# Rotary embedding without a rotation matmul: permuted query and key weight columns in a fused two-layer kernel

## The chip, the cores and the metric

The kernel runs on one core of one Trainium2 chip. The metric is device time in microseconds (us) of one execution, as a median of several. The engines are TensorE (PE, its weight loads PEld), VectorE (DVE), ScalarE (ACT), GpSimd (POOL) and SyncE (SP), which issues the transfers.

## The reference

A first layer blends a memory into the stream; a second one is a transformer layer with two experts per token (self attention, cross attention, feed forward). What the change touches is the projection to queries, keys and values and the rotary embedding (B = 4 batches of S = 512 tokens, D = 512, 16 heads of 32):

```python
vm = expert_mask(token_type_ids)[..., None]
x = rms_norm(hidden_states, ln_in_w)
mixed = jnp.where(vm, x @ v_qkv, x @ l_qkv)
q, k, v = jnp.split(mixed, 3, axis=-1)
q, k, v = (heads(q, NH, HD), heads(k, NH, HD), heads(v, NH, HD))
# rotate_half(x) = concatenate([-x[..., d:], x[..., :d]]), d = 16
q, k = q * cos + rotate_half(q) * sin, k * cos + rotate_half(k) * sin
ctx = sdpa(q, k, v, causal=True)
```

## The kernel before

The whole model is one program on one core, cut into stages by an all-engine barrier (`clear`, L71 to L76): gated_context (L89), queries_values_keys (L689), self attention (from L1143), projections, cross attention, feed forward. Each engine has its own instruction stream, written out by hand in the order in which it runs; semaphores order the engines against each other. Matrix products are made of float32 values split into a rounded high part and a rest: three matmuls per product (`three`, L104 to L108).

The stage queries_values_keys works on one batch per turn, four turns (`turns`, the last batch first). In a turn TensorE runs three phases of eight steps, four for expert 0 and four for expert 1 (`project` and `run`): Q (part 0), V (part 1), K (part 2); the last turn has the order Q, K, V (`place`). A phase fills four of the eight PSUM banks, so that a phase's banks are written again two phases later. Q and K come out transposed, one piece of 128 output features x 512 tokens per bank; V has tokens on the partitions. Expert 1 is computed only for the last 128 tokens if no early token needs it: after the fourth step of Q, TensorE reads a flag and branches (L1138 to L1141) to a wide or a narrow version of the rest of the turn; with these inputs the narrow one runs, and the wide one, which lies before it in the program, is jumped over.

After the fourth step of Q two matmuls (`sums`, L1105) add the squares of the tokens for the norms of the turn. ScalarE makes the roots (`root`), VectorE the scaled tables cos_r and sin_r (`second_sums` L995 and L998, `tables` L1004 to L1007). TensorE's V phase waits for the second of these steps (s_tab at 5i + 2).

The rotary embedding of a piece goes through five engines. ScalarE copies the piece out of PSUM (`keep_plain`, L840). GpSimd multiplies the copy by cos_r (`scale_pieces`, L931), TensorE multiplies it by a constant matrix rot that swaps the halves of each head with the sign (`rotate`, L1097; one matmul in plain float32, four records in the trace, back into the piece's own bank). VectorE multiplies that by sin_r (L1017) and adds both (L1020). ScalarE rounds the sum (`round_piece`, L847; two slots), VectorE takes the rest (L1024), and SyncE stores both (`store_piece`, L754 and L756) as 128 rows of 2 KB. The products with cos_r lie in a ring t1 of three slots. On TensorE the rotations of a turn's Q pieces stand behind the first two steps of its V phase, two per step, and those of its K pieces behind the first two steps of the next turn's Q phase; in the last turn Q's stand in the K phase and K's in the V phase.

VectorE's order in a turn is: `turn_pieces` for the preceding turn's K, `second_sums`, `tables`, `turn_pieces` for this turn's Q, the copy rs_col (L1050) of four transposed columns that TensorE makes at V's fifth step (L1130), then masks, tokens and rests of the next turn (`find_keep`, `mask_x`, `rest_x` L987). The K phase waits for rs_col. In turn 0 the splits of the key weights (`round_w` on ScalarE, `rest_w` on VectorE) stand among these. The query weights of expert 0 are split at the end of the stage before (`split_tile`, L357 to L370).

## Time and profile before

| what | value |
|---|---|
| timed runs | 2179.99, 2180.31 and 2183.4 us, median 2180.31 us |
| profiled execution, span | 2183.6 us |
| TensorE busy | 2022.3 us (93%) |
| VectorE busy | 1492.5 us (68%) |
| ScalarE busy | 1006.7 us (46%) |
| GpSimd busy | 503.2 us (23%) |
| the stage queries_values_keys, from Q's expert 1 of turn 0 to the next stage's first matmul | 389.53 to 623.39 us |

All rows come from one execution that was profiled; for that execution the profile gives the span and no other time. Busy times count work, not waiting. Matmuls are pipelined, their ends are modelled and overlap the following starts, so distances between starts are read rather than durations. PEclk is the clock that TensorE was granted, as a share of full speed. A bracket behind a row gives the idle time of that engine just before it and what ended it. "PEq" and "PEldq" are TensorE's sequencer, "SPq" the queue of SyncE.

### The profile page before, as it was taken

How to read it: one execution, taken by the hardware profiler on the slowest of the kernel's cores; microseconds unless marked ns; L12 is line 12 of the kernel's file. 1: busy time of each engine (PE TensorE's matmuls, PEld its weight loads, DVE VectorE, ACT ScalarE, POOL GpSimd, SP SyncE). 2: the span in 40 equal slices, each digit the busy share in tenths (PEclk: the TensorE clock that was granted, in tenths of full speed). 3: DMA queues.
4: the chain of work that ended last, by engine and by line, in shares of the span. 5: the costliest groups of instructions: out<-in, count | busy, mean ns of one | idle time of the engine just before them, and what ended most of it. 6: DMA issues, size and time to landing. Idle time of an engine off the chain costs nothing. (4 is left out here: it accounts for less than half of the span.)

```text
span 2183.6 us, 32815 instructions
## 1 busy us (share of the span) xinstructions
PE 2022.3 (93%) x12701; PEld 1349.4 (62%) x12718; DVE 1492.5 (68%) x2047; ACT 1006.7 (46%) x1748; POOL 503.2 (23%) x496
## 2 busy tenths in 40 slices
PE   6999997899979997888889999999998899999997
PEld 5788874677755554677634444444434678778885
DVE  5776786566547775656579999999952565866563
ACT  1333314445415554444348888888884222221111
POOL 0321231133301212332201213222132212221211
PEclk9999998799979999999979999999999899999999
DMA  3222112333367662585544354453501433344332
GB/s 139 70 99 80 40 53 86 113 122 122 99 173 171 171 166 87 207 263 195 156 124 84 71 97 83 78 98 69 97 17 26 124 88 102 98 110 112 99 94 58
DMA packets 174936, 236.99 MB, mean 109 GB/s; under 512 B 26234, under 2 KB 103166, under 8 KB 172570
## 3 DMA queue, kind: packets, MB, share of 16 engines
q1 hardware_dynamic: 166624, 223.71, 38.2%
q0 software_dynamic: 7856, 10.90, 1.8%
q8 instruction: 113, 1.85, 0.4%
q14 instruction: 55, 0.45, 0.1%
q10 hardware_dynamic: 288, 0.08, 0.0%
HBM read 169.61 MB, written 62.91 MB: 106 GB/s over the span
## 5 line engine op out<-in xcount | busy, mean ns | idle before, releaser
L2133 ACT ACTIVATE pT_x<-ps 128x512 f32<-128x512 f32 (+1 forms) x832 | 451.3, 595 | 85.3 <-PE ps L2231 57.6
L2172 DVE TENSOR_REDUCE quarters<-ps 128x2 f32<-128x804 f32 x480 | 454.4, 992 | 46.1 <-PE ps L2203 45.0
L2246 PE MATMUL ps<-pT_x,vx_ring 128*17 128x256 f32 (+1 forms) x3328 | 261.9, 388 | 0.2 <-ACT osb_x L2115 0.2
L106 PE MATMUL ps<-mi_h,w_hi 128*128 128x512 f32 (+1 forms) x440 | 174.0, 396 | 10.5 <-DVE mi_l L2427 10.5
L2392 POOL TENSOR_TENSOR sg<-sg,keep_all 128x512 f32<-128x512 f32 (+1 forms) x55 | 87.8, 1595 | 386.5 <-ACT sg L2371 386.5
L107 PE MATMUL ps<-mi_h,w_lo 128*128 128x512 f32 (+1 forms) x440 | 173.4, 394 | 0.0
L108 PE MATMUL ps<-mi_l,w_hi 128*128 128x512 f32 (+1 forms) x440 | 172.8, 393 | 0.0
L1320 DVE TENSOR_REDUCE row_max_s<-ps 128x1 f32<-128x384 f32 (+3 forms) x176 | 109.5, 633 | 67.9 <-PE ps L1352 67.1
L1292 ACT ACTIVATE pT_s<-ps 128x512 f32<-128x512 f32 (+1 forms) x176 | 96.0, 558 | 114.9 <-PE ps L1377 112.8
L100 DVE CAST w_hi<-w_raw 128x512 fp32r<-128x512 f32 (+1 forms) x165 | 84.4, 511 | 71.5 <-PE ps L108 65.5
L2246 PEld LDWEIGHTS ps<-pT_x,vx_ring 128*17 128x17 f32 (+1 forms) x3328 | 55.6, 95 | 110.9 <-issue 68.5
L102 DVE TENSOR_TENSOR w_lo<-w_raw,w_hi 128x512 fp32r<-128x512 f32 (+1 forms) x165 | 115.8, 702 | 5.7
L2375 ACT ACTIVATE hid_h<-prod 128x512 fp32r<-128x512 f32 (+1 forms) x55 | 34.9, 634 | 177.5 <-DVE prod L2455 177.5
L2371 ACT ACTIVATE sg<-ps 128x512 f32<-128x512 f32 (+1 forms) x55 | 32.8, 596 | 164.4 <-PE ps L108 164.4
L291 ACT ACTIVATE pT<-ps 128x512 f32<-128x512 f32 (+1 forms) x52 | 31.0, 598 | 158.0 <-PE ps L108 158.0
L106 PEld LDWEIGHTS ps<-mi_h,w_hi 128*128 128x128 f32 (+1 forms) x440 | 82.3, 187 | 31.0 <-issue 11.5
L1352 PE MATMUL ps<-qkv_h,qkv_l 96*128 96x128 f32 (+3 forms) x256 | 90.5, 414 | 10.1 <-PEq L76 7.8
L108 PEld LDWEIGHTS ps<-mi_l,w_hi 128*128 128x128 f32 (+1 forms) x440 | 82.3, 187 | 20.1
L107 PEld LDWEIGHTS ps<-mi_h,w_lo 128*128 128x128 f32 (+1 forms) x440 | 82.3, 187 | 18.8
L2455 DVE TENSOR_TENSOR prod<-ps,sg 128x512 f32<-128x512 f32 (+1 forms) x55 | 37.9, 690 | 78.8 <-PE ps L108 70.0
L106 PE MATMUL ps<-hid_h,w_hi 128*128 128x512 f32 (+1 forms) x220 | 87.9, 400 | 3.0 <-DVE hid_l L2459 3.0
L331 POOL TENSOR_TENSOR sin_t<-sin_t,pT 128x512 f32<-128x512 f32 (+1 forms) x48 | 72.4, 1509 | 65.0 <-ACT pT L291 64.4
(350 smaller groups left out, 4816.6 us busy)
## 6 DMA issues: line engine op xcount, KB each, us to landing
qkv_l<-self_q_by_part SPq DMA_DIRECT2D x48, 256.0 KB, 4.5
qkv_h<-self_k_by_part SPq DMA_DIRECT2D x48, 256.0 KB, 6.6
w_raw<-L_xattn_l_gate SPq DMA_DIRECT2D x40, 256.0 KB, 2.9
w_raw<-L_xattn_l_up SPq DMA_DIRECT2D x40, 256.0 KB, 2.9
w_raw<-L_xattn_l_down SPq DMA_DIRECT2D x40, 256.0 KB, 2.7
kx_first<-cross_k_by_part SPq DMA_DIRECT2D x36, 200.2 KB, 6.7
cross_v_by_group<-v_aug SPq DMA_DIRECT2D x16, 442.0 KB, 3.8
vx_ring<-cross_v_by_group SPq DMA_DIRECT2D x16, 442.0 KB, 10.0
```

The lines of the kernel that those rows point to most:

```text
L100: nc.vector.tensor_copy(hi, raw).then_inc(s_high, 1)
L102: nc.vector.tensor_tensor(out=lo, in0=raw, in1=hi.bitcast(f32), op=ALU.subtract).then_inc(s_split, 1)
L106: nc.tensor.matmul(dst, ah, bh, start=start, stop=False, **how)
L107: nc.tensor.matmul(dst, al, bh, start=False, stop=False, **how)
L108: return nc.tensor.matmul(dst, ah, bl, start=False, stop=stop, **how)
L1292: nc.scalar.activation(pT[:, u % 3, j:j + n, 0:width], heads_of(ps[:, SCORES + v % 3, :], n, width), ACT.Exp, scale=SCALE).then_inc(s["s_e ...
L1320: nc.vector.tensor_reduce(out=row_max[:, g % 2, j:j + heads, q], in_=heads_of(bank, heads, (q + 1) * P), axis=AX.X, op=ALU.max)\
L1352: last = nc.tensor.matmul(bank[:, m * width:(m + 1) * width], q_r[0:STACK, at + m, cut], k_r[0:STACK, at + m, 0:width], start=False, stop= ...
L2133: nc.scalar.activation(pT[0:kn, u % 3, j, :], ps[0:kn, 5 + v % 3, :], ACT.Exp, scale=SCALE)\
L2172: nc.vector.tensor_reduce(out=quarters[:, g % 2, pair, :, q, quarter], in_=ps[:, at:at + 2, 0:MAXW], axis=AX.X, op=ALU.max)\
L2246: last = nc.tensor.matmul(ps[j * HD:j * HD + CHD + 1, 4, queries], v_r[0:kn, g % RING, kt, j, :], pT[0:kn, u % 3, j, queries], start=kt == ...
L2392: nc.gpsimd.tensor_tensor(out=by_batch(sg[0:cn, c % 2, :]), in0=by_batch(sg[0:cn, c % 2, :]), in1=keep_all[0:cn, experts[i], :, rows(i)], ...
```

## The change

The columns of the query and key weights are permuted when the weights are split into high part and rest. Piece q then holds, for all eight pairs of heads, one half of one head of the pair: pieces 0 and 1 hold the first and second halves of the even heads, pieces 2 and 3 those of the odd heads. What the rotation matmul fetched from 16 partitions further is now in the same partition of the neighbouring bank (j and j ^ 1). VectorE multiplies piece j by cos_r and piece j ^ 1 by sin_r, both straight from PSUM; GpSimd subtracts or adds the two; ScalarE rounds as before, VectorE takes the rest, two pieces behind instead of one. `keep_plain`, `rotate`, the constant rot and its load are gone. The ring t1 has four slots, and VectorE, not GpSimd, now waits for a free slot. A piece is stored as eight blocks of 16 rows, so that the rows in memory are in the old order. The `sums` of a turn and the transposes at V's fifth step wait for the second multiply of two pieces. The value weights keep their order.

```diff
+        def by_piece(w):
+
+            return w.rearrange("p (a q r) -> p q a r", q=DT, r=HD // 2)
...
-                            nc.vector.tensor_copy(hi, w_raw[:, n % RAW, :]).then_inc(s["s_wh"], 1)
+                            raw = w_raw[:, n % RAW, :]
+                            if n >= DT + ET:
+                                raw, hi, lo = by_piece(raw), *(w.rearrange("p (q a r) -> p q a r", q=DT, r=HD // 2) for w in (hi, lo))
+                            nc.vector.tensor_copy(hi, raw).then_inc(s["s_wh"], 1)
                             dve.wait_ge(s["s_wh"], n + 1)
-                            nc.vector.tensor_tensor(out=lo, in0=w_raw[:, n % RAW, :], in1=hi.bitcast(f32), op=ALU.subtract)\
+                            nc.vector.tensor_tensor(out=lo, in0=raw, in1=hi.bitcast(f32), op=ALU.subtract)\
...
+            TR = 4
...
+                def piece_rows(dst, i, part, j):
+
+                    return dst[turns[i], part].rearrange("(a q r) n -> q a r n", q=DT, r=HD // 2)[j]
+
+                def raw_of(n):
+
+                    raw = w_raw[:, n % RAW, :]
+                    return raw if n // G == 1 else by_piece(raw)
+
+                def as_raw(w, n):
+
+                    return w if n // G == 1 else w.rearrange("p (q a r) -> p q a r", q=DT, r=HD // 2)
...
-                            sp.dma_start(dst[turns[i], 0, k * P:(k + 1) * P, :], hi[:, o % 2, :].bitcast(f32)).then_inc(s_uh[o % 2], 16)
+                            sp.dma_start(piece_rows(dst, i, 0, k), hi[:, o % 2, :].bitcast(f32)).then_inc(s_uh[o % 2], 16)
                             sp.wait_ge(s["s_rl"], o + 1)
-                            sp.dma_start(dst[turns[i], 1, k * P:(k + 1) * P, :], t1[:, o % 3, :]).then_inc(s_ul[o % 3], 16)
+                            sp.dma_start(piece_rows(dst, i, 1, k), t1[:, o % TR, :]).then_inc(s_ul[o % TR], 16)
...
-                            nc.scalar.activation(split_of(n)[0], w_raw[:, n % RAW, :], ACT.Copy).then_inc(s["s_wh"], 1)
+                            nc.scalar.activation(as_raw(split_of(n)[0], n), raw_of(n), ACT.Copy).then_inc(s["s_wh"], 1)
...
-                        def keep_plain(i, group):
-
-                            act.wait_ge(s["s_wu"], done(i, 2 * group))
-                            for j in range(DT):
-                                o = 2 * DT * i + DT * group + j
-                                if o >= DT:
-                                    act.wait_ge(s["s_rp"], o - DT + 1)
-                                nc.scalar.activation(plain[:, j, :], ps[:, bank(3 * i + place(i, 2 * group), j), :], ACT.Copy).then_inc(s["s_pl"], 1)
-
                         def round_piece(o):
 
                             act.wait_ge(s["s_rp"], o + 1)
                             if o >= 2:
                                 act.wait_ge(s_uh[o % 2], 16 * (o // 2))
-                            nc.scalar.activation(hi[:, o % 2, :], t1[:, o % 3, :], ACT.Copy).then_inc(s["s_rh"], 1)
+                                act.wait_ge(s["s_rl"], o - 1)
+                            nc.scalar.activation(hi[:, o % 2, :], t1[:, o % TR, :], ACT.Copy).then_inc(s["s_rh"], 1)
...
-                                keep_plain(i - 1, 1)
                                 for j in range(2):
                                     round_piece(2 * DT * (i - 1) + DT + j)
                             root(i, 0)
@@ -890,14 +900,12 @@
                                 for j in range(2, DT):
                                     round_piece(2 * DT * (i - 1) + DT + j)
                             root(i, 1)
-                            keep_plain(i, 0)
                             if i == 0:
                                 for n in range(2 * G, 3 * G):
                                     round_w(n)
                             for j in range(DT):
                                 round_piece(2 * DT * i + j)
                             if i == B - 1:
-                                keep_plain(i, 1)
...
-                        def scale_pieces(i, group):
-
-                            pool.wait_ge(s["s_tab"], 5 * (i + 1))
+                        def join_pieces(i, group):
+
                             for j in range(DT):
                                 o = 2 * DT * i + DT * group + j
-                                pool.wait_ge(s["s_pl"], o + 1)
-                                if o >= 3:
-                                    pool.wait_ge(s_ul[o % 3], 16 * (o // 3))
-                                nc.gpsimd.tensor_tensor(out=t1[:, o % 3, :], in0=plain[:, j, :], in1=cos_r[:, :], op=ALU.mult)\
-                                    .then_inc(s["s_t1"], 1)
+                                pool.wait_ge(s["s_t1"], o + 1)
+                                pool.wait_ge(s["s_t2"], o + 1)
+                                nc.gpsimd.tensor_tensor(out=t1[:, o % TR, :], in0=t1[:, o % TR, :], in1=plain[:, j, :],
+                                                        op=ALU.add if j % 2 else ALU.subtract).then_inc(s["s_rp"], 1)
...
+                            nc.vector.tensor_tensor(out=as_raw(lo_, n), in0=raw_of(n), in1=as_raw(hi_.bitcast(f32), n), op=ALU.subtract)\
...
                         def turn_pieces(i, group):
 
                             dve.wait_ge(s["s_tab"], 5 * (i + 1))
-                            for j in range(DT + 1):
+                            dve.wait_ge(s["s_wu"], done(i, 2 * group))
+                            for j in range(DT + 2):
                                 o = 2 * DT * i + DT * group + j
                                 if j < DT:
-                                    dve.wait_ge(s["s_rot"], o + 1)
-                                    dve.wait_ge(s["s_t1"], o + 1)
-                                    nc.vector.tensor_tensor(out=plain[:, j, :], in0=ps[:, bank(3 * i + place(i, 2 * group), j), :], in1=sin_r[:, :],
-                                                            op=ALU.mult).then_inc(s["s_t2"], 1)
-                                    dve.wait_ge(s["s_t2"], o + 1)
-                                    nc.vector.tensor_tensor(out=t1[:, o % 3, :], in0=t1[:, o % 3, :], in1=plain[:, j, :], op=ALU.add)\
-                                        .then_inc(s["s_rp"], 1)
-                                if j:
-                                    dve.wait_ge(s["s_rh"], o)
-                                    nc.vector.tensor_tensor(out=t1[:, (o - 1) % 3, :].bitcast(f32r), in0=t1[:, (o - 1) % 3, :],
-                                                            in1=hi[:, (o - 1) % 2, :].bitcast(f32), op=ALU.subtract).then_inc(s["s_rl"], 1)
+                                    banks = [ps[:, bank(3 * i + place(i, 2 * group), n), :] for n in (j, j ^ 1)]
+                                    if o >= TR:
+                                        dve.wait_ge(s_ul[o % TR], 16 * (o // TR))
+                                    nc.vector.tensor_tensor(out=t1[:, o % TR, :], in0=banks[0], in1=cos_r[:, :], op=ALU.mult)\
+                                        .then_inc(s["s_t1"], 1)
+                                    if o >= DT:
+                                        dve.wait_ge(s["s_rp"], o - DT + 1)
+                                    nc.vector.tensor_tensor(out=plain[:, j, :], in0=banks[1], in1=sin_r[:, :], op=ALU.mult)\
+                                        .then_inc(s["s_t2"], 1)
+                                if j >= 2:
+                                    dve.wait_ge(s["s_rh"], o - 1)
+                                    nc.vector.tensor_tensor(out=t1[:, (o - 2) % TR, :].bitcast(f32r), in0=t1[:, (o - 2) % TR, :],
+                                                            in1=hi[:, (o - 2) % 2, :].bitcast(f32), op=ALU.subtract).then_inc(s["s_rl"], 1)
...
-                        def rotate(i, group, j):
-
-                            o = 2 * DT * i + DT * group + j
-                            pe.wait_ge(s["s_pl"], o + 1)
-                            nc.tensor.matmul(ps[:, bank(3 * i + place(i, 2 * group), j), :], rot[:, :], plain[:, j, :], start=True, stop=True)\
-                                .then_inc(s["s_rot"], 1)
-
                         def sums(i, n):
 
                             pe.wait_ge(s["s_sum"], 3 * (2 * i + n + 1))
                             if i:
-                                pe.wait_ge(s["s_t2"], 2 * DT * (i - 1) + DT + n + 1)
+                                pe.wait_ge(s["s_t2"], 2 * DT * (i - 1) + DT + 2)
                             nc.tensor.matmul(ps[:, bank(3 * i + 1, n), :], ones[:, :], sq[:, 2 + n, :], start=True, stop=True)\
                                 .then_inc(s["s_ss"], 1)
 
@@ -1109,22 +1111,13 @@
 
                             parts = (0, 2, 1) if i == B - 1 else (0, 1, 2)
                             for m in steps:
-                                step, n = m % G, G * parts[m // G] + m % G
+                                n = G * parts[m // G] + m % G
                                 project(i, n, t0)
-                                if m < 2 and i:
-                                    rotate(i - 1, 1, 2 * m)
-                                    rotate(i - 1, 1, 2 * m + 1)
                                 if m == 3:
                                     sums(i, 0)
                                     sums(i, 1)
-                                if m // G == 1 and step < 2:
-                                    rotate(i, 0, 2 * step)
-                                    rotate(i, 0, 2 * step + 1)
-                                if i == B - 1 and m // G == 2 and step < 2:
-                                    rotate(i, 1, 2 * step)
-                                    rotate(i, 1, 2 * step + 1)
                                 if n == G + 4:
-                                    pe.wait_ge(s["s_t2"], 2 * DT * i + DT * (place(i, 1) - 1) + 1)
+                                    pe.wait_ge(s["s_t2"], 2 * DT * i + DT * (place(i, 1) - 1) + 2)
```

## Rows read from the trace of the kernel before

**Rows 1.** The page: busy us, share of the span and instructions of each engine.

```profile
PE 2022.3 (93%) x12701; PEld 1349.4 (62%) x12718; DVE 1492.5 (68%) x2047; ACT 1006.7 (46%) x1748; POOL 503.2 (23%) x496
```

**Rows 2.** Windows: length, busy (x) of PE, PEld, DVE, ACT, POOL, PEclk, DMA share, GB/s.

```profile
399.80:439.17 39.37, 37.53 (x173) 29.90 (x174) 28.51 (x40) 19.39 (x33) 10.21 (x8) 0.93 0.42 141
439.17:496.74 57.57, 56.85 (x283) 44.54 (x282) 37.97 (x53) 28.53 (x45) 19.95 (x15) 1.00 0.33 116
496.74:554.30 57.56, 56.83 (x283) 44.56 (x282) 37.95 (x52) 28.55 (x45) 19.96 (x15) 1.00 0.33 115
554.30:615.60 61.30, 60.59 (x290) 45.91 (x289) 33.12 (x45) 23.01 (x36) 20.24 (x15) 1.00 0.41 134
615.60:623.39 7.79, 0.04 (x1) 0.05 (x2) 0.00 (x0) 2.42 (x4) 0.00 (x0) 0.82 0.47 139
...
422.50:425.90 3.40, 3.40 (x10) 2.61 (x9) 2.20 (x5) 0.01 (x1) 0.00 (x0) 0.52 0.77 236
```

**Rows 3.** Lines, 399.8 to 616: busy us, mean ns of one, then idle before.

```profile
L1097 PE MATMUL ps<-plain,rot 128*128 128x512 f32 x64 | 30.7, 602 | 2.2 <-ACT plain L840 2.2
```

**Rows 4.** Timeline of TensorE, turn 0, V: start us, us, engine, line, operation.

```profile
402.55 0.39 PE L107 MATMUL ps<-qkv_h,xe0l 128*128 128x512 f32 x1
...
403.69 1.88 PE L1097 MATMUL ps<-plain,rot 128*128 128x512 f32 x4
...
405.64 0.40 PE L107 MATMUL ps<-qkv_h,xe0l 128*128 128x512 f32 x1
```

**Rows 5.** Timeline of TensorE, turn 1: Q, sums, V, V's expert 1, K.

```profile
439.46 0.40 PE L107 MATMUL ps<-xe0h,w_lo 128*128 128x512 f32 x1
...
441.80 0.40 PE L108 MATMUL ps<-xe0l,w_hi 128*128 128x512 f32 x1
...
454.67 1.88 PE L1105 MATMUL ps<-sq,ones 128*128 128x512 f32 x4
...
461.70 0.46 PE L106 MATMUL ps<-qkv_h,xe0h 128*128 128x512 f32 x1
...
476.63 0.39 PE L106 MATMUL ps<-qkv_h,xe1h 128*128 128x512 f32 x1
...
480.55 0.39 PE L106 MATMUL ps<-xe0h,qkv_h 128*128 128x512 f32 x1
```

**Rows 6.** Timeline of TensorE, turn 0: the first matmul of K.

```profile
421.30 0.47 PE L106 MATMUL ps<-xe0h,qkv_h 128*128 128x512 f32 x1 [1.83 <-DVE rs_col L1050]
```

**Rows 7.** Branch and first narrow instruction (ns min/median/max, starts); turn 0's Q, expert 1.

```profile
L1139 PEldq COMPARE_BRANCH  x4: 3312/3530/3811, 382.3 to 567.4; - x4
...
L1068 PEldq EVENT_SEMAPHORE  x4: 51/51/51, 389.4 to 393.4; - x4
...
389.53 0.44 PE L106 MATMUL ps<-xe1h,qkv_h 128*128 128x128 f32 x1 [6.37 <-issue]
```

**Rows 8.** Lines of the pieces' steps on VectorE, GpSimd and ScalarE, 330 to 640.

```profile
L1020 DVE TENSOR_TENSOR t<-t,plain 128x512 f32<-128x512 f32 x32 | 25.8, 807 | 1.1
...
L1017 DVE TENSOR_TENSOR plain<-ps,sin_r 128x512 f32<-128x512 f32 x32 | 21.9, 685 | 32.6 <-POOL t L931 23.9 <-PE ps L1097 8.7
...
L931 POOL TENSOR_TENSOR t<-plain,cos_r 128x512 f32<-128x512 f32 x32 | 43.7, 1386 | 104.2 <-DVE sin_r L1007 39.8 <-ACT plain L840 27.3 <-DMA self_q_by_part<-t 22.0
...
L847 ACT ACTIVATE rows_h<-t 128x512 fp32r<-128x512 f32 x32 | 19.8, 629 | 54.9 <-DVE t L1020 54.9
```

**Rows 9.** Timeline of VectorE, turn 2: last rest of x, last table.

```profile
499.20 1.53 DVE L987 TENSOR_TENSOR xe1l<-full_x,xe1h 128x512 fp32r<-128x512 f32 x1 [0.16 <-ACT xe1h L820]
...
523.23 0.68 DVE L1007 TENSOR_TENSOR sin_r<-sin_t,rs 128x512 f32<-128x512 f32 x1
```

**Rows 10.** Transfers, 340 to 640: count, size, median us to landing.

```profile
self_q_by_part<-rows_h SPq DMA_DIRECT2D x16, 256.0 KB, 2.3
...
qkv_h<-self_k_by_part SPq DMA_DIRECT2D x10, 256.0 KB, 6.8
```

**Rows 11.** Timeline of VectorE, end of the stage before.

```profile
331.21 1.29 DVE L498 COPY h<-ps 128x512 f32<-128x512 f32 x2 [1.79 <-PE ps L108]
```

More of the change, by code:

```diff
@@ L236, in _ @@
                             load_w(sp, n, tiles[n], wl, s["s_ws"])
-                        sp.wait_ge(s["s_pos"], 96)
+                        sp.wait_ge(s["s_pos"], 80)
                         sp.wait_ge(s["s_up"], 16 * (B - 1))
@@ L392, in positions @@
                         def positions():
-                            dve.wait_ge(s["s_pos"], 96)
+                            dve.wait_ge(s["s_pos"], 80)
                             nc.vector.tensor_copy(posf, posi).then_inc(s["s_hot"], 1)
@@ L689, in queries_values_keys @@
         def queries_values_keys(more_h, more_l, k_r, q_r, v_r, s_key, s_value, s_first):
[L691 to L692 removed]
+            names = ("s_tt s_k s_ku0 s_ku1 s_eu s_hin s_x s_xh s_xl s_sq s_sum s_ss s_rs s_tab s_r0u s_t1 s_t2 s_rp s_rh s_rl "
+                     "s_uh0 s_uh1 s_ul0 s_ul1 s_ul2 s_ul3 s_rc s_rcc s_vn s_uv0 s_uv1 s_hup " + WSEMS)
             ctx, sems = stage(names)
@@ L695, in queries_values_keys @@
             wl = [s[f"s_wl{i}"] for i in range(RAW)]
-            s_ku, s_uv, s_uh, s_ul = ([s[f"{n}{i}"] for i in range(k)] for n, k in (("s_ku", 2), ("s_uv", 2), ("s_uh", 2), ("s_ul", 3)))
+            TR = 4
+            s_ku, s_uv, s_uh, s_ul = ([s[f"{n}{i}"] for i in range(k)] for n, k in (("s_ku", 2), ("s_uv", 2), ("s_uh", 2), ("s_ul", TR)))
             weights, GROUPS, G = [t["L1_xattn_l_qkv"], t["L1_xattn_v_qkv"]], (0, 2, 1), 2 * DT
@@ L783, in _ @@
                                     sp.wait_ge(s_uv[m], 16 * ST)
-                                for m in range(3):
-                                    sp.wait_ge(s_ul[m], 16 * len(range(m, 4 * DT, 3)))
+                                for m in range(TR):
+                                    sp.wait_ge(s_ul[m], 16 * len(range(m, 4 * DT, TR)))
                                 self_key_loads(sp, 0, k_r, q_r, s_key)
@@ L803, in _ @@
                             sp.wait_ge(s_uh[m], 16 * DT * B)
-                        for m in range(3):
-                            sp.wait_ge(s_ul[m], 16 * len(range(m, 2 * DT * B, 3)))
+                        for m in range(TR):
+                            sp.wait_ge(s_ul[m], 16 * len(range(m, 2 * DT * B, TR)))
                     @block.scalar
@@ L936, in _ @@
                             if i:
-                                scale_pieces(i - 1, 1)
-                            scale_pieces(i, 0)
+                                join_pieces(i - 1, 1)
+                            join_pieces(i, 0)
                             if i + 1 < B:
                                 add_squares(i + 1)
-                        scale_pieces(B - 1, 1)
+                        join_pieces(B - 1, 1)
                     @block.vector
@@ L967, in rest_w @@
                             dve.wait_ge(s["s_wh"], n - SPLIT + 1)
-                            nc.vector.tensor_tensor(out=lo_, in0=w_raw[:, n % RAW, :], in1=hi_.bitcast(f32), op=ALU.subtract)\
+                            nc.vector.tensor_tensor(out=as_raw(lo_, n), in0=raw_of(n), in1=as_raw(hi_.bitcast(f32), n), op=ALU.subtract)\
                                 .then_inc(s["s_ws"], 1)
@@ L2573, in constants @@
     c = {"c_ident": np.eye(P, dtype=np.float32)}
-    rot = np.zeros((P, P), np.float32)
-    low = p % HD < HD // 2
-    rot[p[low] + HD // 2, p[low]] = -1.0
-    rot[p[~low] - HD // 2, p[~low]] = 1.0
-    c["c_rot"] = rot
     c["c_sel"] = (p[:, None] == np.array([[HD * h for h in range(4)] + [HD * h + CHD for h in range(4)]])).astype(np.float32)
```

6 lines of the change are left out of this document (1 added, 5 removed).

## The prediction

> **What bounds the kernel now.** I read the page's busy times first: TensorE is busy for 2022.3 of the 2183.6 us span, VectorE for 1492.5 [rows 1]. That is an average over stages, so I then cut the one stage that the change rebuilds (queries, values, keys) into its four turns, at each turn's first matmul. The reader is to see the TensorE column: 56.85 of 57.57 us and 56.83 of 57.56 in turns 1 and 2, at full granted clock, with VectorE at 38 and GpSimd at 20 [rows 2]. So TensorE's stream sets the end of every turn, and what leaves that stream is gained if nothing else becomes later than it. The grouped lines give the stream's share that goes: 64 records of the rotation matmul, 30.7 us busy, 2.2 us idle before them waiting for ScalarE's copies [rows 3]. The rows in order of time then give the price in the stream (ends of pipelined matmuls overlap, so I use distances between starts).
>
> **The change part by part.**
>
> *Rotations removed.* Plain matmuls start 0.228 us apart (402.55 to 403.69 is five of them). From the first rotation record at 403.69 to 405.64 are 1.95 us, with one plain matmul inside: a pair of rotations costs 1.95 − 0.23 = 1.72 us [rows 4]. There are 16 pairs (two in turn 0, four in turns 1 and 2, six in turn 3): 16 x 1.72 = 27.5 us. Pairs that also wait cost more; to catch that I build a turn without rotations. Expert 0 of Q is 48 matmuls at 0.234 (439.46 to 441.80 is ten of them): 11.2. From the sums to V's start, 454.67 to 461.70: 7.0. Expert 0 of V, 48 x 0.228: 10.9. V's expert 1 with the transposes, 476.63 to 480.55: 3.9. K, 480.55 to the next turn's first matmul at 496.74: 16.2 [rows 2, 5]. Sum 49.3 against 57.57: **8.2 us in each of turns 1 and 2**, of which 6.9 are pairs and 1.3 their waits. Turn 3 is the same work in another order, and its window ends 0.3 us after its last start: 61.30 − 49.3 − 0.3 = **11.6 us**.
>
> *Turn 0.* Two pairs, 3.4 us. K's first matmul stood 1.83 us for the copy rs_col [rows 6], which is queued on VectorE behind the Q pieces, and these behind the K weights' splits. ScalarE's four copies that stood ahead of those splits are gone, so the splits run while TensorE still works on Q's expert 1; the pieces begin at Q's end (399.8) and need about 9 us, while V takes 14.8. The stall goes: 1.8 us. After it the granted clock fell for 3.4 us to 0.52, that is near 1.2 of 2.4 GHz [rows 2]: (1 − 0.52) x 3.4 = 1.6 us that I expect back, since nothing stands there any more. Last the jump, L1139: the branch over the wide version of the turn takes 3.3 to 3.8 us in all four turns; in turns 1 to 3 the matmuls already queued cover it, in turn 0 TensorE stood 6.37 us, and its stream's first narrow instruction came at 389.4, 7 us after the branch began at 382.3 [rows 7]. So there two waits of that size follow one another. Fewer instructions per turn put the turn's code elsewhere; from 7.1 − 3.8 the second wait is worth up to 3.3 us. Ends 0 and 3.3; I take 1.5, the middle, having no nearer row. Turn 0 in all: 3.4 + 1.8 + 1.6 + 1.5 = **8.3 us**.
>
> *The pieces' new path.* Per piece VectorE did multiply by sin, add, rest; now it does two multiplies from PSUM and the rest: three again. The old multiply reads PSUM too and takes 685 ns [rows 8], so the new ones take that, at 0.62 from start to start: nothing gained or lost in busy time, if two PSUM operands from neighbouring banks cost no more. GpSimd does one operation per piece as before (1386 ns, two SBUF operands, as the join [rows 8]). ScalarE loses 32 copies. What matters is when each wait of TensorE is met.
> K pieces wait only for VectorE: the preceding turn's last x rest ends at 499.20 + 1.53 = 500.73, 4.0 us after the turn's start [rows 2, 9]. The second pair of multiplies, for which sums now wait, ends at 4.0 + 4 x 0.62 = 6.5; sums come at 11.2. Covered by 4.7 us. If that cover were gone, TensorE would wait there with the whole turn behind it.
> Q pieces begin when the tables are done, 523.23 + 0.68 = 523.91 in turn 2; I call this T. V starts at 461.70 + 57.56 = 519.26 in that turn, T − 4.65, so without rotations K starts at T − 4.65 + 10.9 + 3.9 = T + 10.2 [rows 2, 5, 9]. Behind T: multiplies of three pieces to T + 3.7; joins from 1.3 in steps of 1.39 to T + 5.5 for three, the fourth 7.0; piece 1 is rounded by T + 4.8 (0.63 on ScalarE [rows 8]), its store then needs 2.3 us to land [rows 10] before the same slot is rounded for piece 3: T + 7.1, rounded 7.8, rest done 8.6, rs_col 8.8. It is needed at T + 10.2. So **1.4 us of cover**, the thinnest of the change. Gone, it costs its excess in turns 1 and 2.
> The slot wait of the t1 ring moves from GpSimd to VectorE; queued behind it there are the other pieces and rs_col. With four slots it asks for a store issued a whole group earlier: nothing.
>
> *Stores* now write 8 blocks of 16 rows instead of 128 rows, from the same queue, as many as before. The nearest row is the old store, 2.3 us; the far one 6.8 us, a load of the same size [rows 10]. I take 2.3; up to 3.7 nothing is late.
>
> *Weight columns.* Reads of the raw tile in short runs, in 16 splits. The 12 of this stage lie beside TensorE work. Four in the stage before are VectorE casts of 0.42 us, back to back with work for which TensorE waits (1.79 us before L498's copies, 0.65 each [rows 11]). If the short runs cost the cast its speed, 4 x (0.65 − 0.42) = 0.9 us are lost; ends 0 and 0.9, I take **0.4 us lost**. One constant load less: off the path, nothing.
>
> *Sum.* 8.3 + 8.2 + 8.2 + 11.6 − 0.4 = **35.9 us**. The next stage starts 7.79 us after the last window in any case [rows 2]: a barrier, all later work moves as one. The profiled execution's span, 2183.6 us, is 0.2 above the slowest of the timed runs and 3.3 above their median, 2180.31; the rows differ from a timed run by 0.15%, on 36 us nothing. Forecast: 2180.3 − 35.9 = **2144.4 us**.
>
> **The rivals.**
>
> *rs_col comes late.* For: two operations with two SBUF operands now meet oftener, the join on GpSimd and the rest on VectorE, and such VectorE operations are the uneven ones: L1020's mean is 807 ns against 685 for L1017 with one PSUM operand, and one rest beside GpSimd took 1.53 [rows 8, 9]. Against: during most of a join VectorE runs PSUM multiplies. If all four rests took 1.53, the last ends 3.4 us later, 2.0 beyond the cover; with a clock dip as in turn 0, 3.6 a turn, in two turns 7 us: 2151.5.
> The Trainium skill, "GPSIMD Engine Reference", section 1. Specifications, says that GpSimd shares its SBUF interfaces with VectorE and contends with VectorE instructions of two SBUF inputs. By that rule this rival holds in part; the trace agrees in the direction (807 against 685 ns), and the new multiplies are of the kind that it spares.
>
> *The double wait at the jump moves to another turn.* For: code moves in every turn. Against: a turn's waits have to fall together as in turn 0. Then turn 0's 1.5 may turn to 3.3 and another turn pays 3.3 and a dip of 1.6: 2144.4 − 1.8 + 4.9 = 2147.5, or, where turn 0 keeps its own too, 2151.
> The Trainium skill, "Runtime: NRT & Kernel Launch", section Instruction fetch mechanics, says that a taken branch to code outside two 16 KiB blocks forces a fetch before it goes on. By that the second wait would depend on where a block ends; the trace shows the 3.3 to 3.8 us per jump, not the blocks' place in the changed program.
>
> *Slower: the stores land late.* Each group of four pieces has one landing between rounding piece 1 and piece 3. Above 3.7 us every microsecond of landing delays K's start in turns 1 and 2; above some 5 (tables behind the K pieces' last rest) also V's start in turns 1 to 3; turn 0 and the end follow later. With some six groups on the path the loss is about 6L − 26: 6.8 us (the far row) would cost 15 and leave 2159; the sign turns at L near 10.5, and 12 us would give 2190. Blocks of 32 KB speak against so much.
>
> *Nothing gained.* If the pieces' chain replaced TensorE as the bound, a turn would be as long as VectorE's 38 us plus its waits; it would need 11 us of waits to reach 49.3 and 19.5 for today's time [rows 2]; VectorE has 19.6 of idle now, most of it on the rotation's chain. 2180.
>
> **How the numbers follow.** Forecast 0.76, late rs_col 0.10, jump 0.08, late stores 0.04 (half of it with a loss), nothing gained 0.02. Range: below, the jump's second wait wholly gone (−1.8), no cast loss (−0.4), and up to 1.5 for unevenness that the dense turn of plain distances leaves out: 2140.7. Above, the two middle rivals: 2152. A measurement of this kernel can tell about 0.2% (4 us) from no change. Faster 0.95, same 0.02, slower 0.03.
>
> **What would show it.** In the profile after: no L1097; turns 1 and 2 at 49 to 50 us with TensorE over 98% busy; turn 3 near 49.6; no idle before K's first matmul in turn 0 and no low clock behind it; less than 6.4 us of "issue" before Q's expert 1 there; stores landing within 3.7 us. I am wrong if a turn's K starts behind rs_col, if a jump shows a gap in turns 1 to 3, or if the multiplies take over 0.7 us.

## The result: 18.9 us faster, half of what was forecast

The changed kernel takes 2162.0 us (median of four runs, 2161.4 to 2164.3), the kernel before 2180.9 beside it: a ratio of 0.9911, with a 95% interval of 0.9898 to 0.9925. The forecast was 2144.4 us with a range of 2140.7 to 2152.0: the sign was right, the size was not, 35.9 us against 18.9.

The page's busy times after the change:

```profile
PE 1989.5 (92%) x12637; PEld 1334.6 (62%) x12654; DVE 1482.1 (69%) x2047; ACT 991.2 (46%) x1716; POOL 507.3 (23%) x496
```

TensorE has lost 32.8 us of busy time against [rows 1], ScalarE 15.5 us; its 32 copies are gone. The work went, then; the time didn't all follow. The windows by turn, cut as in [rows 2] (turn 0 from V on, turns 1 to 3, the way to the next stage), and a short one behind K's start in turn 2 (length; busy and count of PE, PEld, DVE, ACT, POOL; PEclk; DMA share; GB/s):

```profile
397.21:429.99 32.78, 32.78 (x166) 27.74 (x166) 21.74 (x33) 12.62 (x21) 10.67 (x8) 0.95 0.34 114
429.99:481.21 51.22, 49.61 (x267) 41.58 (x266) 33.69 (x49) 22.86 (x34) 20.62 (x14) 1.00 0.40 129
481.21:536.72 55.51, 51.73 (x267) 42.69 (x266) 38.16 (x56) 26.17 (x39) 21.30 (x15) 0.97 0.37 120
536.72:586.35 49.63, 49.63 (x266) 41.53 (x265) 29.08 (x43) 16.36 (x22) 22.22 (x15) 1.00 0.45 132
586.35:600.46 14.11, 0.00 (x2) 0.06 (x2) 1.46 (x3) 3.68 (x6) 0.00 (x0) 0.58 0.59 193
518.79:524.00 5.21, 5.21 (x16) 4.13 (x17) 3.32 (x8) 1.21 (x2) 0.00 (x0) 0.67 0.73 219
```

Turn 3 has the forecast length (49.63 us against 49.3 + 0.3). Turn 1 is 1.9 us too long, turn 2 6.2 us, and from the last V matmul to the next stage are 14.11 us instead of 7.79 [rows 2]. These three make 14.4 of the 17 us that are missing. TensorE's own rows say what it stood for (timeline of TensorE: K of turns 0 and 1, V of turn 2, K of turn 2):

```profile
413.80 0.39 PE L105 MATMUL ps<-xe0h,qkv_h 128*128 128x512 f32 x1
...
464.93 0.47 PE L105 MATMUL ps<-xe0h,qkv_h 128*128 128x512 f32 x1 [1.61 <-DVE rs_col L1059]
...
501.45 0.50 PE L105 MATMUL ps<-qkv_h,xe0h 128*128 128x512 f32 x1 [1.11 <-DVE rs L1004]
...
518.79 0.47 PE L105 MATMUL ps<-xe0h,qkv_h 128*128 128x512 f32 x1 [2.24 <-DVE rs_col L1059]
```

The stall of [rows 6] is gone in turn 0. New ones stand in front of K in turns 1 and 2, at the place that the prediction called the thinnest cover of the change, and one in front of V in turn 2, for the tables. Behind the one of 2.24 us the granted clock is 0.67 in the mean of 5.2 us (the last window): 1.7 us more.

Why rs_col is late is read in the chain of turn 2's Q pieces, step by step against the prediction's times behind T, the end of the tables (timeline of VectorE, ScalarE and SyncE's queue; L858 rounds a piece, L773 issues the store of its high part):

```profile
505.47 0.68 DVE L1013 TENSOR_TENSOR sin_r<-sin_t,rs 128x512 f32<-128x512 f32 x1
...
510.20 0.63 ACT L858 ACTIVATE rows_h<-t 128x512 fp32r<-128x512 f32 x1 [0.62 <-POOL t L937]
...
511.37 0.56 SPq L773 DMA_DIRECT2D self_q_by_part<-rows_h  x1
...
517.22 0.63 ACT L858 ACTIVATE rows_h<-t 128x512 fp32r<-128x512 f32 x1 [2.80 <-DMA self_q_by_part<-rows_h]
...
518.49 0.15 DVE L1059 COPY rs_col<-ps 128x4 f32<-128x4 f32 x1
```

T is 506.15. Piece 1 is rounded at T + 4.7 (forecast T + 4.8). Its store is issued 0.5 us later, at 511.37, and the slot is free for piece 3 only at 517.22, 5.85 us after the issue, where the forecast had 2.3. Everything after is late by about that: rs_col is done at T + 12.5 instead of T + 8.8, K starts at T + 12.6 instead of T + 10.2.

The stores are the same 256 KB from the same queue. In the transfers' table they have no landing time any more (compare [rows 10]):

```profile
self_q_by_part<-rows_h SPq DMA_DIRECT2D x16, 256.0 KB
```

The reason lies in the trace's completion events. A store of the kernel before raised its semaphore 16 times, one of the changed kernel 9 times: once 1 us after the issue, then 8 times when data has landed. Taking the ninth event as the landing, the 64 stores took 4.06 us at best and 5.2 in the median; before they took 2.0 and 2.3. The Trainium skill, "DMA: Bandwidth & Descriptors", section "Why a DMA increments its semaphore by 16 and not by 1", gives the rule: a transfer from such a queue is shared by as many of the 16 DMA engines, at most, as divide the size of the slowest loop of both access patterns, and the queue writes the rest of the 16 counts at once. Eight blocks of 16 rows have a slowest loop of 8. By that rule eight engines carry what sixteen carried; the nine events and the doubled time agree. The prediction did not draw on this page.

### The profile page after: what moved, and what is told of

Its sections match the earlier page's. It is cut to its first block and busy times, and to the rows that moved or that the text cites. A ratio compares the mean times of both kernels' runs of the same rounds, so it can differ in the third digit from the quotient of the medians.

```text
span 2162.6 us, 32626 instructions
## 1 busy us (share of the span) xinstructions
PE 1989.5 (92%) x12637; PEld 1334.6 (62%) x12654; DVE 1482.1 (69%) x2047; ACT 991.2 (46%) x1716; POOL 507.3 (23%) x496
## 5 line engine op out<-in xcount | busy, mean ns | idle before, releaser
L106 PEld LDWEIGHTS ps<-mi_h,w_lo 128*128 128x128 f32 (+1 forms) x440 | 82.3, 187 | 18.6
```

Of the source, the lines that this page charges most:

```text
L106: nc.tensor.matmul(dst, al, bh, start=False, stop=False, **how)
```

## The experiments

**Is it the stores?** Two runs, each with the stores alone as the difference. In the first the kernel before gets the new blocks:

```diff
-sp.dma_start(dst[turns[i], 0, k * P:(k + 1) * P, :], hi[:, o % 2, :].bitcast(f32)).then_inc(s_uh[o % 2], 16)
+sp.dma_start(dst[turns[i], 0].rearrange("(a q r) n -> q a r n", q=DT, r=HD // 2)[k], hi[:, o % 2, :].bitcast(f32)).then_inc(s_uh[o % 2], 16)
...
```

> The kernel before with one edit: every piece is stored as 8 blocks of 16 rows (the rows then lie in another order in memory; nothing else is changed). Theory S (stores): such a store is finished by fewer DMA engines and lands in 4 to 6 us instead of 2.3, whatever the rest of the kernel does. In the kernel before the Q pieces have about 1.9 us to spare ahead of K's start in turns 1 and 2, so about 1 us a turn is lost there, with a clock dip after each stall, and the last turn's K pieces end late: 2180.5 + 4 to 10, about 2187. Theory C (contention): what is late in the changed kernel is late because GpSimd's joins and VectorE's rests slow each other, the store only stands in the row; then this edit costs under 2 us, 2181.

Measured: 2208.1 us against 2182.4, ratio 1.0115 (1.0091 to 1.0139): 25.7 us slower, two and a half times the upper end of what theory S expected, and far from theory C. The waits of the span 360 to 640 show where the rest is (engine, tile, line, waited for: us in total, times, longest):

```profile
POOL t L931 <- DMA self_q_by_part<-t: 38.2, 6, 14.4
...
POOL t L931 <- DMA self_k_by_part<-t: 27.9, 4, 7.9
```

I had counted the two slots of the high part alone. In the kernel before, GpSimd waits at the head of the pieces' path for a slot of the ring of three; in [rows 8] 22.0 us of its idle time already stood against that landing. Tables, copies and the rotations in TensorE's stream queue behind it.

In the second run the changed kernel gets the old block:

```diff
-return dst[turns[i], part].rearrange("(a q r) n -> q a r n", q=DT, r=HD // 2)[j]
+return dst[turns[i], part, j * P:(j + 1) * P, :]
```

> The changed kernel, but every piece is stored as one block of 128 rows as before the change (the rows then lie in another order in memory). Theory S: landings fall back to 2 to 2.4 us, the stalls at K's start in turns 1 and 2 (1.6 and 2.2 us) and what follows them go: turns 1 and 2 at 49.3 us instead of 51.2 and 55.5, 8 us gained; if the late tail (14.1 us from the last V matmul to the next stage instead of 7.8) is of the same cause, 6 more: 2148 to 2154. Theory C: the stalls stay, 2160 or more.

Measured: 2146.8 us, 35.6 less than the kernel before beside it (2182.4), ratio 0.9839 (0.9817 to 0.9861). The forecast's sum was 35.9. Turns 1 and 2 and the way to the next stage (windows), then the end of turn 2's tables, the rounding of piece 3 and rs_col (timeline), then the store's landing (transfers):

```profile
429.51:479.39 49.88, 49.60 (x266) 41.55 (x266) 36.91 (x52) 24.63 (x37) 21.01 (x15) 1.00 0.38 133
479.39:528.94 49.55, 49.55 (x267) 41.56 (x266) 37.21 (x53) 24.77 (x37) 20.63 (x15) 1.00 0.38 134
...
579.04:586.77 7.73, 0.00 (x1) 0.06 (x2) 0.00 (x0) 2.34 (x4) 0.00 (x0) 0.67 0.47 140
```

```profile
501.64 0.69 DVE L1013 TENSOR_TENSOR sin_r<-sin_t,rs 128x512 f32<-128x512 f32 x1
...
509.87 0.63 ACT L858 ACTIVATE rows_h<-t 128x512 fp32r<-128x512 f32 x1 [1.15 <-POOL t L937]
...
511.14 0.16 DVE L1059 COPY rs_col<-ps 128x4 f32<-128x4 f32 x1
```

```profile
self_q_by_part<-rows_h SPq DMA_DIRECT2D x16, 256.0 KB, 2.3
```

T is 502.33. rs_col is done at T + 9.0 (forecast 8.8) and K starts at 512.75, T + 10.4 (10.2). No K stands: theory C falls.

**Is it the number of blocks?** Two more kernels change that number alone. Four blocks of 32 rows:

```diff
-return dst[turns[i], part].rearrange("(a q r) n -> q a r n", q=DT, r=HD // 2)[j]
+return dst[turns[i], part].rearrange("(a q r) n -> q a r n", q=DT, r=HD)[j]
```

> The changed kernel with pieces stored as 4 blocks of 32 rows (the rows then lie in another order in memory). Theory S: half as many engines share a store as with 8 blocks, so a store alone lands in about 8 us instead of 4.1, and the slot waits of ScalarE and VectorE grow by 3 to 4 us a pair: each of turns 1 to 3 longer by 8 to 15 us, in all 2185 to 2215. If the number of blocks did not matter: 2162.

Measured: 2222.6 us, ratio 1.0186 (1.0168 to 1.0204), slower than the kernel before and above the expected range. At best a store lands in 6.1 us, not 8, with five events instead of nine. K now waits for 6.0 and 4.7 us in turns 1 and 2, and the second phase of turns 2 and 3 for the tables, 2.3 us each (timeline of TensorE, K of turn 1, V and K of turn 2); `sums`, which the prediction had seen covered, wait 6.9 us in turns 1 to 3 together:

```profile
483.63 0.76 PE L105 MATMUL ps<-xe0h,qkv_h 128*128 128x512 f32 x1 [5.99 <-DVE rs_col L1059]
...
530.13 0.79 PE L105 MATMUL ps<-qkv_h,xe0h 128*128 128x512 f32 x1 [2.29 <-DVE rs L1004]
...
552.51 0.53 PE L105 MATMUL ps<-xe0h,qkv_h 128*128 128x512 f32 x1 [4.67 <-DVE rs_col L1059]
```

And sixteen blocks of 8 rows, in the right place, with another order inside a piece:

```diff
 def by_piece(w):
-    return w.rearrange("p (a q r) -> p q a r", q=DT, r=HD // 2)
+    return w.rearrange("p (a q r) -> p q r a", q=DT, r=HD // 2)
...
-return dst[turns[i], part].rearrange("(a q r) n -> q a r n", q=DT, r=HD // 2)[j]
+return dst[turns[i], part].rearrange("(a q r) n -> q r a n", q=DT, r=HD // 2)[j]
...
-angle = np.tile(angle, (1, 2 * P // HD))
+angle = np.repeat(angle, 2 * P // HD, axis=1)
```

> The changed kernel with another order inside a piece: partition 8r + a instead of 16a + r holds row r of head pair a (the split of the weights, the store and the order of the frequencies in the table follow). Each piece then goes to its right place as 16 outer blocks of 8 rows. Theory S, the number of outer blocks sets how many DMA engines share a store: landings of 2 to 2.5 us and the time of the kernel that stores one block, about 2147. If the rows' distance were what is slow: landings over 4 us, about 2162 or more. The reads of the raw weights now step 64 elements; if that slows the four casts of the stage before, under 1 us is lost.

Measured: 2156.0 us, ratio 0.9882 (0.9865 to 0.9898): 6 us better than the changed kernel and 26 better than the one before, the fastest kernel here that puts every row in its place; still 9 us behind the one-block run. Stores (transfers) and the turns (windows: 1, 2, 3, the way to the next stage):

```profile
self_q_by_part<-rows_h SPq DMA_DIRECT2D x16, 256.0 KB, 3.1
```

```profile
437.88:487.24 49.36, 49.36 (x267) 41.66 (x266) 35.53 (x52) 23.85 (x36) 20.67 (x14) 1.00 0.44 134
487.24:536.65 49.41, 49.41 (x266) 41.66 (x266) 36.31 (x52) 24.42 (x36) 20.96 (x14) 1.00 0.44 134
536.65:586.30 49.65, 49.63 (x266) 41.52 (x265) 31.89 (x48) 18.38 (x26) 22.38 (x15) 1.00 0.56 159
586.30:594.10 7.80, 0.00 (x1) 0.06 (x2) 0.00 (x0) 2.42 (x4) 0.00 (x0) 0.67 0.58 176
```

Every one of them is the forecast's. So rows that lie 64 apart do little harm. The shortest landing of a run goes with its number of blocks: 6.1 us with 4, 4.1 with 8, 2.8 with 16; one block of 128 rows takes 2.0. The last two both raise their semaphore 16 times; what parts them is open. What this kernel loses comes earlier: turn 0's first matmul stands at 364.14 us instead of 357.39. Two of these 6.75 us are there before the first split (it begins at 316.02 us instead of 314.05; over all kernels here between 313.7 and 317.1), the other 4.8 come behind it. The splits now read single elements 64 apart (lines by form, 300 to 420; the changed kernel's cast, then this run's rounding on ScalarE and its cast):

```profile
L372 DVE CAST w_hi<-w_raw 128x512 fp32r<-128x512 f32 x4 | 1.7, 420 | 0.0
```

```profile
L831 ACT ACTIVATE qkv_h<-w_raw 128x512 fp32r<-128x512 f32 x20 | 18.0, 921 | 2.0 <-DMA w_raw<-L_xattn_v_qkv 1.9
...
L372 DVE CAST w_hi<-w_raw 128x512 fp32r<-128x512 f32 x4 | 3.5, 886 | 0.0
```

The cast's mean doubles, from 420 to 886 ns (at the least 418 and 601), and VectorE takes 2.4 us more from the first split to the last. TensorE waits 2.1 us for it, and behind that the clock is at half from 329.5 us on for 6.8 us, where the changed kernel's execution has full clock. ScalarE's roundings begin only behind the first matmul: 921 ns is a mean of eight value tiles at 0.61 to 0.67 us, read as before, and twelve permuted ones at 1.08 to 1.19; in the changed kernel all twenty take 0.61 to 0.63. So runs of 16 elements had cost neither engine anything. The expectation had allowed under 1 us for the longer steps; that was wrong.

**Where does the late tail come from?** ScalarE, VectorE and SyncE's queue at the end of the changed kernel's turn 3, and the next stage's first matmul:

```profile
586.77 0.63 ACT L858 ACTIVATE rows_h<-t 128x512 fp32r<-128x512 f32 x1 [10.45 <-DMA self_k_by_part<-rows_h]
...
590.53 0.15 DVE L1059 COPY rs_col<-ps 128x4 f32<-128x4 f32 x1
...
591.48 1.91 SPq L812 DMA_DIRECT2D self_v_by_group<-v_nat  x2
...
600.46 0.88 PE L1345 MATMUL ps<-qkv_h,qkv_l 96*128 96x128 f32 x2 [14.11 <-PEq L75]
```

The first four stores of the last turn's K pieces are queued behind seven loads for the next stage and land after 9.4 to 10.6 us (by the completion events); the rounding of piece 2 waits 10.45 us for that, rs_col comes 4.2 us after the last V matmul, and the values are scaled and stored that much later. The next run moves the loads behind these stores:

```diff
+for j in range(DT):
+    store_piece(2 * DT * i + DT + j)
 self_key_loads(sp, 0, k_r, q_r, s_key)
 self_value_load(sp, 0, v_r, s_value)
...
-for j in range(DT):
-    store_piece(2 * DT * i + DT + j)
```

> The changed kernel (8 blocks of 16 rows) with one move on SyncE: in the last turn the next stage's first loads are issued behind the four stores of K pieces, not ahead of them. Theory S2: the late tail (14.1 us between the last V matmul and the next stage instead of 7.8) comes from those stores, shared by fewer engines, queueing behind seven loads (9.4 to 10.6 us to land); then the landings there fall to 4 to 6 us, ScalarE's 10.4 us wait goes, the tail is 8 to 10 us and the time 2157 to 2159, if the loads, 5 us later, are still in time. If the tail came from the V stores or the barrier itself: 2162.

Measured: 2165.7 us, ratio 0.9933 (0.992 to 0.9946): nothing gained on the changed kernel, 3.7 us more by the medians, at the edge of what can be told apart (six runs of 2163.3 to 2172.3 us against four of 2161.4 to 2164.3). The stores of the K pieces land after 4.1 to 6.0 us, as expected; the tail did not shrink (ScalarE; SyncE's queue; TensorE):

```profile
580.29 0.63 ACT L858 ACTIVATE rows_h<-t 128x512 fp32r<-128x512 f32 x1 [2.98 <-DMA self_k_by_part<-rows_h]
...
590.99 4.58 SPq L812 DMA_DIRECT2D self_v_by_group<-full_x  x2
...
602.61 0.66 PE L1345 MATMUL ps<-qkv_h,qkv_l 96*128 96x128 f32 x1 [15.13 <-PEq L75]
```

Now the V stores stand behind the seven loads, land after 8.0 to 9.1 us instead of 3.9 to 5.2, and the stage ends with them. Theory S2 named the right queue, but not the right remedy: in this queue whatever stood last landed late. With faster stores in the old order the tail is 7.73 and 7.80 us. The profiled execution also has a turn 3 of 52.6 us, with a stall of 0.99 us for the tables and 3.4 us at half the clock behind it; that this comes from the move is not shown.

**What is TensorE's part alone?** The rotations are left out of the kernel before; nothing takes their place, so sin multiplies the unrotated piece:

```diff
-dve.wait_ge(s["s_rot"], o + 1)
...
-def rotate(i, group, j):
...
```

> The kernel before with the 32 rotation matmuls left out and nothing else (VectorE multiplies the unrotated piece by sin; the copies, the order of the pieces' path and the stores are those of before). It measures TensorE's part of the change alone. By the prediction's sum the pairs with their waits are 31.4 us in all; but the old path of the pieces is longer, rs_col is ready 12.1 us behind the tables where K could start 10.2 behind them, so 2 us and a clock dip of 1.6 come back in turns 1 and 2, and turn 0's stall grows by the 3.4 us of its two pairs: 2180.5 - 31.4 + 3.4 + 7.2, about 2160. If TensorE's stream were not the bound, the time would fall by less than 10 us.

Measured: 2169.7 us, ratio 0.9931 (0.9906 to 0.9956): 12.7 us of the 35.6 that the one-block run gains. The direction is as expected, the gain smaller by 10 us. TensorE stands where the old, longer path of the pieces ends, and behind the jump (timeline of TensorE: K of turn 0, Q's expert 1 of turn 1, K of turn 2; then the window of turn 1):

```profile
417.57 0.77 PE L106 MATMUL ps<-xe0h,qkv_h 128*128 128x512 f32 x1 [4.52 <-DVE rs_col L1049]
...
450.19 0.32 PE L106 MATMUL ps<-xe1h,qkv_h 128*128 128x128 f32 x1 [1.64 <-issue]
...
527.17 0.47 PE L106 MATMUL ps<-xe0h,qkv_h 128*128 128x512 f32 x1 [1.66 <-DVE rs_col L1049]
```

```profile
435.42:491.52 56.10, 54.46 (x266) 46.12 (x266) 37.80 (x53) 28.69 (x45) 20.32 (x15) 0.91 0.34 118
```

Turns 1 and 3 take 56.1 and 56.5 us. Behind the jump's gaps (1.64 and 1.73 us) the clock is at half for 10.24 us in each, 5.1 us lost: gap and clock are what these turns have over 49.3 and 49.6. The jump begins 0.8 to 1.0 us behind VectorE's second multiply of the preceding K pieces, for which `sums` wait (in turn 1 this ends at 444.25, the branch begins at 445.23); in the one-block run that multiply is done more than 2 us before the jump. So the pieces' path reaches TensorE through the jump too, and two thirds of the gain are gone unless it gets shorter as well. This run's path already leaves out the step through TensorE; of the old one it keeps ScalarE's copy, GpSimd's multiply ahead of VectorE's two steps and the ring of three slots. Which of these counts, and what a shorter path is worth with the rotations still in TensorE's stream, was not tested.

**Turn 0's stall.** Two runs put the rounding of the key weights back behind turn 0's Q, on the kernels with 16 blocks and with one block:

```diff
 if i == 0:
+    act.wait_ge(s["s_wu"], done(0, 0))
     for n in range(2 * G, 3 * G):
         round_w(n)
```

> The same as the run with 16 outer blocks, with one wait more: ScalarE begins to round the key weights only when turn 0's Q is complete, as it did before the change. It measures the turn 0 terms of the sum. If the stall at K's first matmul came from these splits standing ahead of the pieces, 1 to 3 us of idle return there, with a low clock of some 1.6 us behind it: 3 to 4.5 us slower than the run with 16 outer blocks, no other turn changed. If the stall had another cause: no difference.

> The changed kernel with one-block stores (rows in another order in memory), and ScalarE begins to round the key weights only when turn 0's Q is complete, as before the change. The run with 16 outer blocks and this wait showed K's first matmul of turn 0 late by 4.9 us in its profiled execution, but a median no different from its partner's; its weight splits were slowed by the long steps in the raw tile, here they are not. If the turn 0 terms of the sum are right: K's first matmul stands 1 to 3 us, a low clock of about 1.6 us follows, and the time is 2146.8 + 3 to 4.5 us, 2150 to 2151. If they are not: 2147 and no stall in the profile.

With 16 blocks: 2156.7 us, ratio 0.988 (0.9864 to 0.9897), no different from 2156.0 without the wait, although its profiled execution shows a stall (first row below). That execution was the longest of the four, 2165.3 us against 2155.0 to 2157.8; what the others did can't be read. With one block: 2146.8 us, ratio 0.9841 (0.9828 to 0.9854), the same as without the wait, and in the profile half a microsecond of idle with the clock at 1.00 behind it (second row):

```profile
428.02 0.77 PE L105 MATMUL ps<-xe0h,qkv_h 128*128 128x512 f32 x1 [4.06 <-DVE rs_col L1060]
```

```profile
415.19 0.47 PE L105 MATMUL ps<-xe0h,qkv_h 128*128 128x512 f32 x1 [0.55 <-DVE rs_col L1060]
```

So the earlier splits were not what removed the stall of [rows 6]; the shorter path of the pieces does it nearly alone. The splits' order decides only when they are slow themselves.

**One block and the right place.** The last kernel pairs heads 0 to 7 and 8 to 15, stores one block, and lets the next stage's loads put the halves together:

```diff
...
 for r, part in enumerate(parts):
-    sp.dma_start(ring[r * HD:(r + 1) * HD, 4 * i:4 * i + 4, :].bitcast(f32),
-                 src[b, part, rows, :].rearrange("(j d) n -> d j n", d=HD)).then_inc(s_key[i], 16)
+    rows = src[b, part].rearrange("(q a r) n -> q r a n", q=DT, r=HD // 2)
+    for half in range(2):
+        p0 = r * HD + half * HD // 2
+        sp.dma_start(ring[p0:p0 + HD // 2, 4 * i:4 * i + 4, :].bitcast(f32),
+                     rows[m // 2 * 2 + half][:, m % 2 * 4:m % 2 * 4 + 4, :]).then_inc(s_key[i], 16)
...
```

> A version that keeps both gains: pieces pair heads 0 to 7 (pieces 0, 1) and 8 to 15 (pieces 2, 3); each piece is stored as one block of 128 rows, and the next stage gathers a head's two halves with two loads of 16 rows instead of one of 32 (12 loads of 128 KB per group instead of 6 of 256 KB). The weights are split in runs of 16 elements, two instructions per tile. If the store's block count is all that the changed kernel lacks: this stage as with one-block stores (turns 1 and 2 at 49 to 50 us, tail 7.8 us), 2147 to 2150 in all, if the loads, twice as many, stay off the next stage's path. Rival: the loads of 16 rows are issued or land late; then the next stage, 229.6 us from first to last matmul with one-block stores, grows by what TensorE waits for them, 2152 or more.

Measured: 2183.4 us, ratio 1.0002 (0.9987 to 1.0017): all of the gain is given back. Its turns 1 and 2 have 49.8 and 49.6 us, its tail 9.7; the next stage grows from 229.6 to 262.9 us. The rival had the place and a small part of the price. Waits of TensorE from 590 to 860, then the transfers of a small row, of the one-block run and of this one:

```profile
PE ps L1377 <- DMA qkv_l<-shift_by_head: 18.6, 10, 5.2
...
PE ps L1352 <- DMA qkv_h<-self_k_by_part: 8.7, 2, 5.4
```

```profile
shift_by_head<-shift_s SPq DMA_DIRECT2D x15, 8.0 KB, 1.7
```

```profile
shift_by_head<-shift_s SPq DMA_DIRECT2D x14, 8.0 KB, 4.1
```

TensorE waits 8.7 us for key loads (1.6 in the one-block run) and 18.6 us (0.6) for a small row that it needs at once. This row is written and read back through the same queue, behind twelve loads instead of six, and takes 4.1 us to land instead of 1.7. The loads' own medians hardly change, 4.6 and 7.1 us against 4.6 and 6.8, for half the bytes each.

## Why the prediction failed, point by point

| step | forecast, us gained | changed kernel | one-block stores |
|---|---|---|---|
| splits of the stage before | −0.4 | +1.1 | +1.5 |
| turn 0, sums to the next turn | 8.3 | 8.1 | 8.2 |
| turn 1 | 8.2 | 6.4 | 7.7 |
| turn 2 | 8.2 | 2.1 | 8.0 |
| turn 3 | 11.6 | 11.7 | 11.2 |
| way to the next stage | 0 | −6.3 | 0.1 |
| all stages after | 0 | −1.9 | 4.2 |

The columns are differences of starts between the profiled executions. Up to rounding they add to the spans' differences, 21.0 and 40.8; by the medians it is 18.9 and 35.6. The last row is hardly the change's: from the end of self attention on, where no edit reaches, the executions of all kernels here take 1324 to 1330 us, and self attention itself is 1.6 us longer in the changed kernel and 0.9 shorter with one-block stores.

- *Weight columns*: 0.4 us were allowed for the casts of the stage before, and nothing was lost; the cast kept its 420 ns. From the first split to the next stage's first matmul are 41.8 us in the kernel before and in the run with four blocks, which splits as the changed kernel does; the changed kernel's own 43.3 have 3.4 us at half the clock in them (from 339.3).
- *Rotations, and the turn built without them*: right. 49.3 us were forecast, 49.36 and 49.41 stand in the run with 16 blocks, 49.63 (49.6) in turn 3 of the changed kernel. Two of the prediction's differences are a tenth low (57.57 − 49.3 is 8.3, and 61.30 − 49.3 − 0.3 is 11.7), which changes nothing.
- *The multiplies from PSUM*: right, two neighbouring banks cost nothing. VectorE and GpSimd in the changed kernel (lines by form, 330 to 640):

```profile
L1025 DVE TENSOR_TENSOR t<-ps,cos_r 128x512 f32<-128x512 f32 x32 | 21.8, 680 | 2.3 <-DMA self_q_by_part<-t 1.9 <-PE ps L107 0.2
L1029 DVE TENSOR_TENSOR plain<-ps,sin_r 128x512 f32<-128x512 f32 x32 | 21.6, 676 | 0.0
...
L937 POOL TENSOR_TENSOR t<-t,plain 128x512 f32<-128x512 f32 x32 | 46.5, 1472 | 67.3 <-DVE plain L1029 67.2
```

- *Turn 0*: the sum was right, 8.1 for 8.3, one reason was not: it is the shorter path, not the order of the splits, that removed the stall. The jump's term was right in size, by luck: 1.5 was the middle between two ends, taken without a row. Its second wait has moved 3.3 us down the stream and has shrunk (timeline of TensorE, Q's expert 1):

```profile
385.33 0.45 PE L105 MATMUL ps<-xe1h,qkv_h 128*128 128x128 f32 x1 [3.27 <-issue]
...
388.61 0.26 PE L106 MATMUL ps<-xe1h,qkv_l 128*128 128x128 f32 x1 [1.56 <-issue]
```

  3.27 + 1.56 = 4.83 us of idle against 6.37 [rows 7]: 1.5 gained. Of the rival's gap in another turn only 0.43 us showed here, in turn 2; the run without rotations had 1.64 and 1.73.
- *Stores*: this is the step that failed. "The nearest row is the old store, 2.3 us [...] I take 2.3": the row of a store with another loop order was no bound for it; it landed in 4.1 to 10.6 us, 5.85 where K's start hung on it. With the old store in its place 35.6 us of the 35.9 came. The far end of that step, 6.8 us, held the median of 5.2.
- *The rival of late stores* named the mechanism, the place and the landing from which it hurts (3.7 us); its chance of 0.04 was far too low, since "blocks of 32 KB speak against so much" looked at the size of a block and not at the number of blocks. Its price was low too: 6L − 26 gives 5 us at 5.2, the one-block run puts it at 15. It left out the clock behind a stall (1.7 us), and the tail, where the stores queue behind loads (6.3 us); the prediction had said that the end would follow later than the turns.
- *rs_col late* came true as a stall, but not for its reason: GpSimd's join takes 1472 ns against 1386 for the scaling before, 0.3 us over four pieces, and with one-block stores rs_col was done at T + 9.0, against 8.8.

Not settled: slots for four high parts, which would take the landing out of the path, were not tried.

## What to carry over

When a change rewrites the access pattern of a transfer, cost that transfer anew, even where its bytes and its queue stay the same: count its outer blocks before taking over an old landing time. A gain on the engine that bounds the time is only kept if the path that refills its buffers gets shorter as well; measure the two halves apart. And in one queue, moving a transfer out of somebody's way can put it into somebody else's.

## What the runs showed of the hardware

- The shortest landing among the 64 stores of 256 KB was 6.1, 4.1 and 2.8 us with 4, 8 and 16 outer blocks, and 2.0 us with one block of 128 rows.
- VectorE's cast of 128 x 512 elements takes 0.42 us when it reads runs of 16 elements, and 0.60 us when it reads single ones 64 apart (one of four took 1.7; casts of whole rows beside it went up to 1.5 too). The Trainium skill, "SBUF — State Buffer", section "Door 1: The DMA port swizzle", speaks of lines of 16 bytes, and of a penalty for each access that goes to a new one; both rows agree, as runs of 16 elements fill whole lines.
- A stall of 1.6 us in front of K (turn 1) left the clock at 1.00 for the rest of the turn, one of 2.24 us (turn 2) was followed by 3.4 us at 0.50. The length of the stall alone does not tell: with the loads behind the stores, 2.17 us at the same place left the clock at 1.00, and without the rotations 1.64 us behind a jump was followed by 10.2 us at 0.50 (1.2 of 2.4 GHz).
